# Two attention images on one core: the second query chunk's split, image 1's mean, norms and bias in another order, a clearing that waits, and side jobs spread wider

## The reference

```
match_in = prelu(W1 x + b1)                      # 16 channels, 48 x 48
ref      = prelu(W2 mean_2x2(x) + b2)            # 16 channels, 24 x 24
embed_w  = prelu(Wa x + ba)                      # 32 channels
w  = patches3x3(ref);  wn = w / max(sqrt(sum(w*w)), 1e-4)     # 576 keys
xp = patches3x3(match_in)                                      # 2304 queries
yi = softmax over keys(10 * wn . xp)
yd = (conv(tconv(yi, patches6x6(embed_w)), Wd, stride 2) + bd) / 6
x1 = x + yd
out = x1 + dct2(groupnorm(x1))
```

## Time and profile before

| | us |
|---|---|
| median of 3 runs (242.5 to 242.75) | 242.66 |
| the profiled execution | 243.28 |
| its span, first to last instruction | 241.5 |
| busy: PE, DVE, POOL, ACT | 187.8, 169.2, 114.0, 104.4 |
| first scores begin | 32.34 |
| maximum of tile 0 begins | 37.39 |
| first turn begins (step 9) | 78.14 |

### The profile page before, as it was taken

The page is one execution under the profiler, slowest core; times in us unless marked ns, Lnnn a source line. Parts: engine busy times, 40 slices in busy tenths (PEclk is TensorE's granted clock), DMA queues, the critical chain, the costliest instruction groups (busy, mean ns, idle before and its releaser), DMA issues.

```text
span 241.5 us, 3419 instructions
## 1 busy us (share of the span) xinstructions
PE 187.8 (78%) x1140; PEld 154.0 (64%) x1140; DVE 169.2 (70%) x343; ACT 104.4 (43%) x185; POOL 114.0 (47%) x109
## 2 busy tenths in 40 slices
...
GB/s 162 218 117 14 75 119 119 57 110 197 0 0 54 80 0 7 131 24 77 48 100 50 0 4 0 1 3 75 22 48 94 5 0 3 0 0 50 100 0 49
...
## 3 DMA queue, kind: packets, MB, share of 16 engines
...
q10 hardware_dynamic: 400, 0.52, 0.8%
...
## 4 chain that ended last, share of the span: by engine, by line
PE 50%; DVE 24%; ACT 9%; issue 8%; DMA 4%; SPq 2%; ACTq 1%; POOL 0%; DVEq 0%; POOLq 0%
PE zt L806 14%; PE yt L822 13%; PE ps L785 10%; DVE negm L1216 5%; ACT nt L975 4%; PE pm L842 3%; DVE bnst L1038 3%; DVE v L1246 3%; DVE ys L1231 3%; DMA par<-params 2%; DVE mimg L1125 2%; DMA v<-mimg 2%; ACT slanted L930 2%; PE pm L832 2%; SPq L414 1%
## 5 line engine op out<-in xcount | busy, mean ns | idle before, releaser
L594 POOL TENSOR_TENSOR nt<-nt 128x599 f32<-128x599 f32 (+1 forms) x54 | 73.7, 1365 | 49.6 <-ACT nt L983 39.9
L806 PEld LDWEIGHTS zt<-ident,nt 128*125 128x125 f32 (+1 forms) x420 | 54.6, 181 | 15.2 <-issue 2.7
L806 PE MATMUL zt<-ident,nt 128*125 128x128 f32 (+1 forms) x420 | 57.7, 279 | 0.9 <-POOL nt L594 0.9
L822 PE MATMUL yt<-ys,ek 125*128 125x384 f32 (+1 forms) x120 | 50.7, 504 | 5.6 <-DVE ys L1231 5.5
L983 ACT ACTIVATE nt<-nt,rps 128x599 f32<-128x599 f32 x36 | 28.7, 796 | 30.2 <-DVE rps L1223 30.1
L1231 DVE COPY ys<-zt 125x384 f32<-125x384 f32 (+1 forms) x60 | 32.6, 553 | 10.2 <-PE zt L806 6.5
L975 ACT ACTIVATE nt<-ps,negm 128x576 f32<-128x576 f32 x32 | 23.7, 739 | 36.2 <-DVE negm L1216 36.2
L785 PE MATMUL ps<-wh,mh 128*128 128x288 f32 x64 | 19.6, 392 | 14.3 <-DVE mr L1211 6.9
L1216 DVE TENSOR_REDUCE negm<-ps 128x1 f32<-128x576 f32 x32 | 24.1, 752 | 7.5 <-PE ps L785 6.9
L1246 DVE SCALAR_TENSOR_TENSOR v<-yt,v 32x384 f32<-32x384 f32 (+3 forms) x48 | 26.3, 547 | 2.5 <-PE yt L822 1.0
L822 PEld LDWEIGHTS yt<-ys,ek 125*128 125x128 f32 (+1 forms) x120 | 18.6, 192 | 9.2 <-DVE ys L1231 9.0
...
(10 more groups left out here) (150 smaller groups left out, 270.9 us busy)
## 6 DMA issues: line engine op xcount, KB each, us to landing
...
```

Source lines behind the costliest of these rows:

```text
L594: pool.tensor_tensor(nt[:, dst, (to + 1) * KP + 1:(to + 1) * KP + 1 + n], nt[:, one, (row1 + 1) * KP + 1:(row1 + 1) * KP + 1 + n], nt[:, o ...
L806: last = nc.tensor.matmul(turned_thirds(zt[:, m % 2, :], n, col), keys_at(tile, r + dr, n, shift), ident[:, :], start=at == 0, stop=at == ...
L822: nc.tensor.matmul(yt[:, k % 2, 0:CHUNK], ek[b][0:n, blk, :], ys[0:n, blk, :], start=blk == 0, stop=blk == KB - 1).then_inc(s_mb, 1)
```

## The change

- In `BEFORE`: `bias_1` of image 0 stands ahead of image 1's statistics (`xs`) and of `conv2`; the eight `conv1` run without a break; `norm` comes behind all eight instead of behind six; image 1's `mean` comes behind `inorm` instead of between two `conv1`; only chunk 0 is split there.
- Chunk 1's split joins the steps, at third 1: on ScalarE behind tile 1's exponential, on VectorE behind tile 1's maximum and image 1's weights.
- `SPREAD`: `conv1` of image 1 starts at third 12 with pace 2.2 (11 with 1.5 before), so its last part falls into step 9 instead of step 7; `norm` moves from third 25 to 29, `inorm` from 30 to 34, `keys` from 34 to 38, `bias_a` of image 1 from 34 to 37; `conv2` gets pace 2; the other jobs move by one to three thirds.
- Of the three copies of chunk 0's ninth taps one goes from ScalarE's queue to SyncE's, between the patches of chunk 0 and of chunk 1.
- GpSimd waits for the first scores before it clears the shifted tiles and writes the output weights.

```diff
@@ BEFORE
-    ("xs", 0, (0,)), ("mean", 0, (0,)), ("weights", 0, (0,)), ("bias_2", 0, (0,)), ("xs", 1, (0,)), ("conv2", 0, (0, 1)),
-    ("squares", 0, (0,)), ("bias_1", 0, (0,)), ("conv1", 0, (0, 1)), ("mean", 1, (0,)), ("conv1", 0, (2, 3, 4, 5)),
-    ("norm", 0, (0,)), ("conv1", 0, (6, 7)), ("inorm", 0, (0, 1)),
-    ("ninth", 0, (0,)), ("keys", 0, (0, 1)), ("split", 0, (0, 1))]
+    ("xs", 0, (0,)), ("mean", 0, (0,)), ("weights", 0, (0,)), ("bias_2", 0, (0,)), ("bias_1", 0, (0,)), ("xs", 1, (0,)),
+    ("conv2", 0, (0, 1)), ("squares", 0, (0,)), ("conv1", 0, (0, 1, 2, 3, 4, 5, 6, 7)), ("norm", 0, (0,)), ("inorm", 0, (0, 1)),
+    ("mean", 1, (0,)), ("ninth", 0, (0,)), ("keys", 0, (0, 1)), ("split", 0, (0,))]
@@ SPREAD
-    ("bias_a", 0, 1, 5, 1), ("squares", 1, 1, 6, 1), ("emb", 0, 2, 7, 2), ("conv1", 1, 8, 11, 1.5), ("ek", 0, 2, 14, 2),
-    ("norm", 1, 1, 25, 1), ("inorm", 1, 2, 30, 2), ("wst", 1, 1, 31, 1), ("keys", 1, 2, 34, 3), ("bias_a", 1, 1, 34, 1),
+    ("bias_a", 0, 1, 6, 1), ("squares", 1, 1, 7, 1), ("emb", 0, 2, 8, 2), ("conv1", 1, 8, 12, 2.2), ("ek", 0, 2, 16, 4),
+    ("norm", 1, 1, 29, 1), ("inorm", 1, 2, 34, 2), ("wst", 1, 1, 34, 1), ("keys", 1, 2, 38, 3), ("bias_a", 1, 1, 37, 1),
...
-    starts += [(3 * TPC * g - SPLIT_LEAD, "split", g // NCH, g % NCH) for g in range(2, NG)]
+    starts += [(max(3 * TPC * g - SPLIT_LEAD, 1), "split", g // NCH, g % NCH) for g in range(1, NG)]
...
+                    if b == 0 and t == 0:
+                        at = 1 + 2 * CHUNK + SHIFTS[2][0]
+                        sp.dma_start(v2[0:CR, 0:CHUNK], mimg[64:64 + CR, at:at + CHUNK]).then_inc(s_nin[0], 16)
...
             perform(before, handlers)
+            pool.wait_ge(s_sc, 1)
             shifted_tiles(DOWN0, 1)
...
-                for n in range(3):
+                for n in (1, 2):
```

4 lines of the change are left out of this document (2 added, 2 removed).

## The result

| | before | changed |
|---|---|---|
| median, us | 242.59 (242.5 to 242.75) | 239.44 (238.56 to 243.53) |
| the profiled execution, us | 243.28 | 238.56 |
| its span, us | 241.5 | 236.8 |

The ratio is 0.9857, 95% interval 0.9808 to 0.9906: 1.4% faster. The prediction was 239.3 us with 236.0 to 243.2. The sum came out right, in part by luck: at tile 11's maximum the change is 1.3 us later than forecast, and the steps behind give 1.3 more than forecast; and one part of the change, the new order ahead of the first tile, is itself a loss, which only the experiments show. In five of the 14 profiles the stretch behind tile 24's maximum lasted 4.3 to 4.8 us longer than the usual 101.6, so profiles are compared up to that maximum, and the ratios leave slow executions out.

The account below looks back on a forecast made before the run. Bounds: a late DMA in the prologue, a VectorE-ScalarE loop in the filling, TensorE behind 100 us. Lead 5.3 at tile 10, 2.4 after step 9, 3.5 after step 12, taken as 3.4: 242.66 - 3.4 = 239.3 us, range 236.0 to 243.2.

Parts of the forecast that it names:

- M: Prologue: end of the match image's (mimg's) edges, at 25.34 us before, forecast at 23.3 (22.6 to 23.8).
- The second part: Prologue: image 1's mean and the norm sums leave the conv1 run, edges 0.8 to 1.4 us earlier; bias_1 costs 0.35.
- First scores at M + 10.0: Prologue: the operations between the edges and tile 0's scores sum to 10.0 us; with faster spreads, scores forecast at 33.1.
- Chunk 1's split: First tiles: with the split behind the maxima, image 1's weights start at 38.1 against 39.13, a lead of 1.0 us.
- The split itself fits: First tiles: VectorE's rests of the moved split end at 41.7, before tile 2's scores do at 42.0.
- Clearing beside the filling: GpSimd's clearing from about 35 to 40.5 beside VectorE's rests: price taken as 0, at worst 0.5 us.
- DMA moves: Prologue queues: moving one ninth-tap copy from ScalarE to SyncE puts nothing on the path.
- Filling: Tiles 2 to 10: stretch by stretch, mainly 3.4 us saved from tile 6 to 7, lead 5.3 at tile 10's maximum.
- Step 9: Tile 10's maximum to the end of tile 11's scores: 6.8 us against 3.9, 2.9 lost, lead 2.4.
- Steps 10 to 12: Behind step 9: spreads leaving step 10 give 1.5 us, their return in 11 and 12 costs 0.4; lead 3.5.
- The slower case: Rival: step 9 takes more than the filling saved, if the lead at tile 10 is under 4.2; 244.0 us, chance 0.18.
- The case of no change: Rival: prologue gains nothing, tile 6 to 7 saves only 2.3, step 9 takes the lead; 242.6 us, chance 0.13.
- The clock case: Rival: a denser filling holds TensorE's upper clock level, 6.1 us faster, 236.6 us, chance 0.14.

Follow-up runs that it names:

- run 2: The kernel before with only the new table of jobs (SPREAD); ratio to before 0.991 (0.9828-0.9991), tile 24's maximum 128.57 us behind wb.
- run 3: The kernel before with only GpSimd's clearing made to wait for the first scores; one execution, tile 24's maximum 128.28 us behind wb.
- run 11: The changed kernel with the old order ahead of the first tile; one execution, tile 24's maximum 124.48 us behind wb.
- run 4: The changed kernel itself, first profile; ratio to before 0.9857 (0.9808-0.9906), tile 24's maximum 127.21 us behind wb.
- run 10: The changed kernel with only image 0's norm put back behind six conv1; ratio to before 0.9787 (0.971-0.9865), tile 24's maximum 124.47 us behind wb.
- run 12: The same kernel as run 11, now timed; ratio to before 0.9729 (0.9685-0.9773), tile 24's maximum 124.84 us behind wb.
- run 8: The changed kernel with chunk 1's split back ahead of the first tile; ratio to before 0.9785 (0.9721-0.985), tile 24's maximum 125.28 us behind wb.
- experiment 3: Same as run 8: the changed kernel with chunk 1's split back ahead of the first tile; ratio to before 0.9785 (0.9721-0.985).
- experiment 1: The changed kernel with the old table of jobs (SPREAD); ratio to before 0.9924 (0.984-1.0009), tile 24's maximum 129.58 us behind wb.
- experiment 2: Same as run 2: the kernel before with only the new table of jobs; ratio to before 0.991 (0.9828-0.9991).

## Why the prediction came out right, and where it was wrong

- **M, the end of the edges: right in size, wrong in its parts.** Forecast 2.0 earlier, measured 2.4 behind `wb` (16.19 to 13.75). The clearing's part was to be 0.96 and is 1.29 (run 2 to run 3). The second part, 0.8 to 1.4 less 0.35 for taking the mean and the norm out of the `conv1` run, is 0.17 (run 11 to run 4): the norm out of the run gives 0.65 (run 10 to run 4), the mean's and the bias' places take 0.48 back (run 11 to run 10). The missing 0.99 came from before's own execution, whose `conv1` products took 1.25 a pair; against such an execution of the old order the second part is worth 1.54 (run 12 to run 4). I had read a run's own length as the cost of what stood between its parts.
- **First scores at M + 10.0: right.** 31.77 - 21.70 = 10.07. The step that failed is the choice of what to compare it with. I noted that the norm gains nothing from being behind, and that the scores come later; I did not work out the chain with the norm left where it was. It gives M + 6.2 to 6.5 (runs 10 and 11) and 2.7 us at tile 24: the reordering is a loss, and the change gained in spite of it.
- **Chunk 1's split: lead 1.0 forecast, 1.29 measured at tile 2, for the wrong reason.** "The split itself fits" assumed the rests done before tile 2's scores. These came at the higher clock and were done at 39.2; the rests, the weights of the embedding and the maximum followed, 40.55. With M earlier and the scores later, the taps were no longer late: the prediction has them landing at about 33.5 and the first scores at 33.1, and never held the one against the other. Measured, they are there at M + 10.4 and the scores begin at M + 10.1 (run 8), and where it was the split would have cost 0.35 at tile 0 and nothing behind it (experiment 3).
- **Clearing beside the filling: price 0, right.** The rests took 0.69 and 0.67, both within the second clearing (38.77 to 40.37), against 0.65 and 0.66 alone; beside one of GpSimd's additions, which read, a rest took 1.74 (73.20 in the changed kernel). The Trainium skill's rule quoted in the prediction holds here. The same section of the Trainium skill (SBUF — State Buffer, Who interferes with whom) says that casts and copies which use the second port pair are blocked for as long as a GpSimd instruction holds it. The trace agrees: the cast at 29.47 ended at 31.18, the clearing beside it at 31.03.
- **DMA moves: "nothing on the path" holds for the changed kernel alone.** In the old order the issue that left ScalarE's queue is worth 0.78 at the first scores (20.91 in run 3, 20.13 in run 11): ScalarE's first copy of the keys starts 1.37 behind the scaling instead of 2.29.
- **Filling: right step by step.** Counted from `wb`, the lead at tiles 4, 6, 7, 8 and 10 is 0.60, 1.41, 4.84, 4.26 and 5.78; forecast 0.7, 1.2, 4.6, 3.8 and 5.3. The 3.4 of tile 6 to 7 is exact, and experiment 1 takes it away again. But step 9 takes the whole of what the table saves here (experiments 1 and 2).
- **Step 9: right to the scores, short by one wait.** Forecast 6.8 us to the end of tile 11's scores, measured 7.3; lead there 2.4 as forecast. But the maximum, not the scores, hands on, and the two copies stood in front of it: lead 1.08. I had counted them as gone from step 8 and not as arriving in step 9, beside GpSimd's additions.
- **Steps 10 to 12: +1.1, right in sum only.** The copies' 1.4 came back at once (tile 11 to 12 in 3.08 us), tile 13 to 14 saved 2.2, and tiles 14 to 16 gave 2.7 back with the embeddings and keys that now stand there. The end lead is 3.51; the forecast was 3.5.
- **The rivals.** The slower case needed a lead under 4.2 at tile 10; it was 5.78, and step 9 took 4.7 of it, so the margin was 1.1. The case of no change needed the stretch from tile 6 to 7 to save only 2.3; it saved 3.4. The clock case did not come: the granted clock is 0.62 to 0.84 from tile 7 to tile 11. Its reason was not what the rows show either: ahead of the two stretches at 0.50 TensorE was busy 3.31 of 4.40 us and 2.82 of 5.30, which is not little.

What stays open: when the `conv1` products become fast. In every profile the first of them take 1.16 to 1.28 us a pair (the two that one part shows in the trace) and the later ones 0.65 to 0.70; the step from one to the other comes anywhere from about 13 us (run 10) to about 19 (before). Later in before a pair takes 1.25 where the granted clock reads 0.50 (at 61.90) and 0.65 where it reads 1.00 (at 51.94), so the lower of TensorE's two levels is the likely reason for the longer time, but it is not shown: up to 21 us the clock reads 1.00 in all 14 profiles. In the new order the first four pairs are done (15.2 in the changed kernel) before the first prelu of `conv1` begins (15.69, waiting for ScalarE), so their speed is off the path, and the edges end at 13.75 behind `wb` in all six profiles (14.40 in run 10, where `norm` stands between); in the old order, with the clearing out of the way, they end anywhere from 13.9 to 15.3.

## What to carry to other kernels

When a chain of small dependent steps (sum, power, spread, scaling) stands ahead of the first tile, start it as early as its input allows and let the big products run beside it; clearing the way for the big products made them end 0.2 us earlier (0.65 by the norm alone) and the chain 3 later. Before moving work out of the way of a late transfer, ask whether another part of the same change makes the transfer early, and weigh the parts together. Where the first product of a new stage queues behind the last of an old one, price the bank it waits for: here moving that product a step forward made one step 4.1 us shorter and the end 2.1 earlier.

## What the runs showed of the chip

- A cast of 16x288 took 0.30 us alone and 1.71 beside GpSimd's clearing, a copy of 96x336 took 0.33 alone and 1.36 to 1.54; a subtraction of two tiles (the rests of a split) took 0.65 to 0.69 alone and beside the clearing. Beside GpSimd's additions the copies took up to 1.62.
- Three DMA issues on ScalarE's queue lasted 2.13 us in the trace (run 3) and two 1.21 (run 11), and the engine's next copy started 0.1 behind them.
- The parameters' load, which starts at 2.6 us wherever a chain shows it, took between 3.92 and 5.11 us, which moves the whole execution by up to 1.2 us.
